# Bidirectional GRU over normalised images: statistics one image ahead of their scales, weight scaling on VectorE, three images summed raw, a shorter order decision

## What is computed

```python
# x: (16, 32, 32, 128) float32, B images of H x W tokens of C channels
xn = (x - mean(x, -1)) / sqrt(var(x, -1) + 1e-5) * ln_gamma + ln_beta
gray = xn.mean(-1)
gp = pad(gray, 1, mode='reflect')
grad_h = resize(abs(gp[..., 2:] - gp[..., :-2]))       # back to 32 x 32
grad_v = resize(abs(gp[..., 2:, :] - gp[..., :-2, :]))
scores = [avgpool3_mean(g) for g in (grad_h, grad_v, (grad_h + grad_v) / 2, abs(grad_h - grad_v))]
logits = relu(scores @ mlp_w1.T + mlp_b1) @ mlp_w2.T + mlp_b2
idx = argmax(softmax(logits))                          # per image
seq = where(idx == 1, columns_first(xn), rows_first(xn))   # (B, 1024, 128)
z = seq @ in_w.T + in_b
yf = gru(z @ wih_f.T + bih_f, whh_f, bhh_f)            # 1024 steps forward
yb = gru(z @ wih_b.T + bih_b, whh_b, bhh_b)            # 1024 steps backward
out = x + concat(yf, yb) @ out_w.T + out_b
```

## Time and profile before

| | |
|---|---|
| median of 3 runs | 1676.18 us (1672.85 to 1676.67) |
| profiled execution, its own time | 1678.4 us |
| its span, first to last instruction | 1676.6 us |
| PE busy / DVE busy / ACT busy / POOL busy | 1609.8 / 1441.4 / 1152.9 / 52.7 us |
| mean granted TensorE clock | 0.522 |
| first sigmoid of the recurrence starts | 85.19 |

### The profile page before, as it was taken

How to read it: one execution, slowest core, us unless ns; L and a number is a source line. 1 busy time by engine, 2 the same in 40 slices (tenths; PEclk the granted TensorE clock), 3 DMA queues, 4 the chain that set the end, 5 groups by cost and what they waited for, 6 DMA issues and landing times.

```text
span 1676.6 us, 61286 instructions
## 1 busy us (share of the span) xinstructions
PE 1609.8 (96%) x21671; PEld 1203.5 (72%) x21671; DVE 1441.4 (86%) x8900; ACT 1152.9 (69%) x6226; POOL 52.7 (3%) x142
## 2 busy tenths in 40 slices
PE   6799999999999999999999999999999999999997
PEld 3477777777777777777777777777777777777775
DVE  6789999888888888888888888888888888888887
ACT  6766666666666666666666666666666666666666
POOL 6500000000000000000000000000000000000000
PEclk9855555555555555555555555555555555555555
DMA  5200000000000000000000000000000000000000
GB/s 177 77 15 12 12 15 12 14 13 12 15 12 12 15 12 15 12 12 15 12 12 8 13 14 12 13 13 12 15 12 13 13 11 15 12 13 13 11 14 17
DMA packets 40359, 31.28 MB, mean 19 GB/s; under 512 B 3576, under 2 KB 37880, under 8 KB 40056
## 3 DMA queue, kind: packets, MB, share of 16 engines
q1 hardware_dynamic: 40056, 27.35, 5.6%
HBM read 18.95 MB, written 8.39 MB: 16 GB/s over the span
## 4 chain that ended last, share of the span: by engine, by line
DVE 68%; ACT 21%; issue 7%; PE 2%; POOL 1%; DMA 0%; SPq 0%; DVEq 0%; POOLq 0%
DVE state L926 31%; ACT drive L530 21%; DVE bank L915 18%; DVE halves L935 12%; DVE big L907 3%; DVE seq L891 2%; DVE xin L907 1%; POOL xin L401 1%; DVE drive L942 1%; PE bank L560 1%; PE bank L552 1%; DMA gamma_row<-in_gamma 0%; ACT seq L455 0%; PE bank L652 0%; ACT big L460 0%
## 5 line engine op out<-in xcount | busy, mean ns | idle before, releaser
L652 PEld LDWEIGHTS bank<-halves,wsplit 128*128 128x128 f16 x18432 | 648.4, 105 | 396.7 <-DVE halves L935 289.2
L652 PE MATMUL bank<-halves,wsplit 128*128 128x16 f16 x18432 | 834.3, 181 | 39.7 <-DVE halves L935 36.2
L926 DVE TENSOR_TENSOR_SCAN state<-gain,drive 128x48 f32<-128x48 f32 x2048 | 526.7, 257 | 165.2 <-ACT drive L530 15.4
L652 PE MATMUL bank<-seq,wcomb 128*128 128x128 f32 x1536 | 592.9, 482 | 2.9 <-DVE seq L891 2.9
L530 ACT ACTIVATE drive<-bank 128x16 f32<-128x16 f32 x2048 | 395.9, 193 | 267.5 <-DVE bank L915 3.0
L524 ACT ACTIVATE rpair<-bank 128x16 f32<-128x16 f32 x2048 | 380.3, 186 | 225.3 <-PE bank L652 225.3
L915 DVE TENSOR_TENSOR_SCAN bank<-rpair,bank 128x32 f32<-128x32 f32 x2048 | 453.1, 221 | 3.4 <-ACT rpair L524 3.4
L935 DVE SCALAR_TENSOR_TENSOR halves<-state 128x32 f16<-128x32 f32 x2048 | 402.9, 197 | 35.5
L527 ACT ACTIVATE gain<-bank 128x16 f32<-128x16 f32 x2048 | 394.1, 192 | 0.0
L652 PEld LDWEIGHTS bank<-seq,wcomb 128*128 128x128 f32 x1536 | 386.0, 311 | 3.1 <-DVE seq L891 3.1
L942 DVE SCALAR_TENSOR_TENSOR drive<-gain,state 128x16 f32<-128x16 f32 x2046 | 365.8, 179 | 0.0
(11 more groups left out here) (104 smaller groups left out, 186.9 us busy)
## 6 DMA issues: line engine op xcount, KB each, us to landing
xin<-in_x SPq DMA_DIRECT2D x16, 512.0 KB, 3.5
big<-in_x SPq DMA_DIRECT2D x96, 64.0 KB
out<-big SPq DMA_DIRECT2D x96, 64.0 KB
xin<-in_x SPq DMA_DIRECT2D x32, 64.0 KB
out<-xin SPq DMA_DIRECT2D x32, 64.0 KB
wih<-in_wiht SPq DMA_DIRECT2D x2, 384.0 KB, 5.9
con<-in_consts SPq DMA_DIRECT2D x1, 572.0 KB
whh<-in_whht SPq DMA_DIRECT2D x2, 192.0 KB, 7.0
```

The lines of the kernel that those rows point to most:

```text
L652: return nc.tensor.matmul(o, w, m, start=start, stop=True, skip_group_check=True)
L926: v.tensor_tensor_scan(state[:, d, ring, :], gain[:, e, cols], drive[:, e, cols], 0.0, ALU.mult, ALU.subtract).then_inc(state_ready[d], 1)
```

## The change

The diff has five groups of edits.

1. DVE's queue is statistics(n), scales(n-1) up to image 12. ACT's `deviation` moves one image further ahead, deviation(n+2).
2. N_PE is 13: images 13, 14 and 15 are summed raw, each between its statistics and its scales. The copy of gray rows is cut into two halves of 512, and stands one image earlier in ACT's queue. The last image is normalised in its own slot.
3. The squares, the high and low parts and `wcomb` move from ACT to DVE, the middle part from the decision phase to the image phase.
4. Decision: halo edges are a multiplication by a column of constants on DVE instead of two products; one bitwise operation takes the absolute value from PSUM; waits among the taps are loosened; the bias b2 is a 33rd row of the product; ACT loads the Exp table ahead of the biases; transposes(15) come behind the resize product in PE's queue; some PSUM banks change.
5. Start of the recurrence: `select` in four pieces of 8 tokens, the fills of a direction wait for its own piece, and the first step does no products on the zero state.

```diff
-N_PE = 14
+N_PE = 13
...
         act.wait_ge(eps_set, 1)
-        act.activation(table[:, :], eps[:, :], ACT.Sqrt)
-        deviation(0)
+        act.activation(table[:, 0:1], eps[:, :], ACT.Sqrt)
+        for n in range(2):
+            deviation(n)
...
         for n in range(B):
             normalise(n)
-            if n == N_PE + 1:
-                act.wait_ge(gray_mm, N_PE)
-                act.copy(gray_rows[:, :], pair[2][0:B, :]).then_inc(gray_copied, 1)
             if n > 0:
                 evacuate_rows(n - 1)
-            if n < B - 1:
-                deviation(n + 1)
+            if n + 2 < B:
+                deviation(n + 2)
             if n > 0:
                 evacuate_columns(n - 1)
-            if n == 4:
-                act.wait_ge(whh_in, 16 * N_REC)
-                act.activation(square[:, :], w_all, ACT.Square, accum_out=sums[:, 0:1]).then_inc(square_set, 1)
+            if n == N_PE:
+                for k in range(2):
+                    act.wait_ge(gray_mm, 2 * N_PE - 1 + k)
+                    act.copy(gray_rows[:, 512 * k:512 * (k + 1)], bank[4 + k][0:B, :]).then_inc(gray_copied, 1)
...
-            if n == 9:
-                act.wait_ge(scale_set, 1)
-                act.activation(parts[0], w_all, ACT.Identity, scale=sk[:, 0:1]).then_inc(high_set, 1)
-            if n == 10:
-                act.activation(parts[2], w_all, ACT.Identity, scale=sk[:, 1:2]).then_inc(weights_set, 1)
-            if n in (11, 12):
...
+        act.activation(table[:, 1:2], eps[:, :], ACT.Exp)
         act.wait_ge(bias_mm, 1)
...
-        for n in range(B):
+        for n in range(B - 1):
             transposes(n)
...
         one(halo[:, 0, :], matrix(C_LEFT), gray[:, :, TPP])
-        one(halo[:, 0, :], matrix(C_LEFT_EDGE), gray[:, :, 2], start=False)
-        one(halo[:, 1, :], matrix(C_RIGHT), gray[:, :, 1])
-        one(halo[:, 1, :], matrix(C_RIGHT_EDGE), gray[:, :, TPP - 1], start=False).then_inc(halo_mm, 1)
+        one(halo[:, 1, :], matrix(C_RIGHT), gray[:, :, 1]).then_inc(halo_mm, 1)
...
-        pe.wait_ge(seq_set, 2 * B)
+        transposes(B - 1)
+        pe.wait_ge(seq_set, 2 * B - 2)
         pooled(0, horiz, first=True)
...
-            if base + r > 0:
-                pe.wait_ge(halves_ready[d], base + r)
+            if base + r == 0:
+                return
...
+        for d in range(2):
+            pe.wait_ge(select_edge, d + 1)
+            if d == 1:
+                pe.wait_ge(reset_and_hn[0], 2)
+            fill_input(0, 0, G_R, d).then_inc(reset_pre[d], 1)
+            fill_input(0, 0, G_N, d).then_inc(reset_and_hn[d], 1)
+            if d == 1:
+                pe.wait_ge(update_ready[0], 1)
+            fill_input(0, 0, G_Z, d).then_inc(update_pre[d], 1)
         pe.wait_ge(select_done, 1)
-        for g in (G_R, G_N, G_Z):
-            fill_input(0, 0, g, 0)
-        for g in (G_R, G_N, G_Z):
-            fill_input(0, 0, g, 1)
...
+        def weight_parts():
+            w_all = whh[:, :, :].rearrange("p d n -> p (d n)")
+            parts = [wsplit[:, k].rearrange("p d n -> p (d n)") for k in range(3)]
+            v.tensor_scalar(parts[0], w_all, sk[:, 0:1], None, ALU.mult).then_inc(high_set, 1)
+            v.tensor_scalar(parts[2], w_all, sk[:, 1:2], None, ALU.mult)
+            dve.wait_ge(high_set, 1)
+            v.scalar_tensor_tensor(out=parts[1], in0=w_all, scalar=sk[:, 0:1], in1=parts[0],
+                                   op0=ALU.mult, op1=ALU.subtract).then_inc(weights_set, 1)
+
+        statistics(0)
+        for n in range(1, B + 1):
+            if n < N_PE:
+                statistics(n)
+                scales(n - 1)
+            if n == N_PE:
+                scales(n - 1)
+            if N_PE <= n < B:
+                statistics(n)
...
+                raw_gray_sums(n)
+                scales(n)
+            if n == 4:
...
+                v.scalar_tensor_tensor(out=square[:, :], in0=flat, scalar=1.0, in1=flat, op0=ALU.mult, op1=ALU.mult,
+                                       accum_out=sums[:, 0:1]).then_inc(square_set, 1)
+            if n == 9:
+                weight_scale()
+            if n == 10:
...
+                weight_parts()
+            if n == 11:
+                for d in range(2):
+                    v.tensor_scalar(wcomb[:, d, :], bank[6 + d][:, 0:3 * HID], sk[:, 0:1], None, ALU.mult).then_inc(fold_set, 1)
...
-        select(0, EDGE)
-        select(L - EDGE, L).then_inc(select_done, 1)
+        select(0, TB).then_inc(select_edge, 1)
+        select(L - TB, L).then_inc(select_edge, 1)
+        select(TB, EDGE)
+        select(L - EDGE, L - TB).then_inc(select_done, 1)
```

More of the change, by code:

```diff
@@ L146, in build @@
     eps = sb("eps", [P, 1])
-    table = sb("table", [P, 1])
+    table = sb("table", [P, 2])
     con = sb("con", [P, C_END])
@@ L247, in build @@
     terms_set = sem("terms_set")
+    taps_set = sem("taps_set")
     high_set = sem("high_set")
@@ L629, in pooled @@
                 at = C_POOL + (which * TPP + j) * 4
-                ins = one(bank[2][0:4, 0:B], con[:, at:at + 4], values[:, :, j], start=first and j == 0)
+                ins = one(bank[0][0:4, 0:B], con[:, at:at + 4], values[:, :, j], start=first and j == 0)
             return ins
-        pe.wait_ge(seq_set, 2 * B)
+        transposes(B - 1)
+        pe.wait_ge(seq_set, 2 * B - 2)
         pooled(0, horiz, first=True)
@@ L644, in _ @@
         pe.wait_ge(scores_set, 1)
[L645 removed]
+        one(bank[1][0:32, 0:B], mlp1[:, :], scores[:, :]).then_inc(hid_mm, 1)
         pe.wait_ge(terms_set, 1)
[L647 to L648 removed]
+        one(bank[1][:, P:P + 4 * B], ones[0:33, :], terms[:, :, :].rearrange("k c b -> k (c b)")).then_inc(logits_mm, 1)
+        pe.wait_ge(seq_set, 2 * B)
         def mm(o, w, m, start=False):
@@ L842, in _ @@
         dve.wait_ge(halo_mm, 1)
-        v.tensor_copy(gray[:, :, 0::TPP + 1].rearrange("p b e -> p e b"),
-                      bank[5][:, 0:2 * B].rearrange("p (e b) -> p e b", e=2)).then_inc(halo_set, 1)
-        dve.wait_ge(halo_set, 1)
+        for e in range(2):
+            v.scalar_tensor_tensor(out=gray[:, :, e * (TPP + 1)], in0=gray[:, :, 2 + e * (TPP - 3)],
+                                   scalar=con[:, C_EDGE + e:C_EDGE + e + 1], in1=bank[5][:, e * B:(e + 1) * B],
+                                   op0=ALU.mult, op1=ALU.add).then_inc(halo_set, 1)
+        dve.wait_ge(halo_set, 2)
         link(v.tensor_tensor(across, gray[:, :, 2:TPP + 2], gray[:, :, 0:TPP], ALU.subtract))
```

133 lines of the change are left out of this document (57 added, 76 removed).

## The result

| | before | after |
|---|---|---|
| median of 17 runs each | 1675.88 us (1672.85 to 1677.76) | 1678.94 us (1677.44 to 1682.85) |
| ratio, 95% interval | | 1.0024 [1.0016, 1.0031] |
| profiled execution, own time | 1678.4 us | 1679.76 us |
| its span | 1676.6 us | 1677.9 us |

The change makes the kernel slower, by 4.0 us by the ratio and 3.1 by the medians, 0.24% and less than the 0.3% that one measurement can tell from no change. The forecast was +1.6.

The account below looks back on a forecast made before the run. Only the start of the recurrence, which runs unchanged on VectorE and ScalarE, can move: image phase +4.0, decision phase -1.0 - 0.2 - 1.6 + 0.4, sum +1.6, so 1677.8 us on the median; range 1672 to 1681.5.

Parts of the forecast that it names:

- mark: Second forward step's matmuls in the recurrence, at 86.51 us before; forecast to move +1.6, with everything after it unchanged.
- ring of four slots: Image phase: scales wait for next statistics, its load and transposes three images back; 10.5 us for three images, 3.5 each.
- short start: Mask's end to the mark: smaller select, fewer fills, no products on zero states; 3.7 us instead of 5.3, -1.6.
- lies 2.2 above the median: Profiled execution of before, 1678.4 us, against median 1676.18; the +1.6 was applied to the median, giving 1677.8.
- T0: T0 to T15 are the starts of each image's transposes on TensorE; T0 is 12.28 us in the profile of before.
- T9 49.5: Image phase: image 9's transposes start at 49.5 us, the last start listed under the ring of four slots.
- The scaled copies: Weight work on VectorE: two copies of 768 elements, taken at 0.93 us each; about 0.5 by the skill page.
- -1.0: Decision phase, halo start to scores copy: 5.7 us instead of 6.7, with TensorE's own queue the long way.
- +0.4: Before ScalarE's first sigmoid: register load and branch take 1.3 to 1.4 us with 1.0 idle left, 0.4 exposed.
- The load is not the limit: Faster rival: statistics never wait for loads and VectorE's own work decides the image phase; -5.8, about 1670.4 us; chance 0.12.
- The image phase breaks even: Rival: ring and raw sums cost half of the forecast, the tail pays; +2.0 - 2.4, 1675.8 us; chance 0.24.
- TensorE stays slow or falls early: Slower rival: late full clock or a fall at 57 in the image phase; 1681 us, or 1684; chance 0.15.

Follow-up runs that it names:

- second profiles: Kernel before and changed kernel, both unedited, run and profiled again; changed kernel's ratio to before 1.0021, mark 86.17 against 85.22.
- six slots: Changed kernel with six slots for images instead of four; ratio to the kernel before 1.0004.
- old images with the new tail: Changed kernel without look-ahead, weight work on ScalarE, two images raw, scale chain at its old place; ratio to the kernel before 0.9974.
- the last kernel: Old images with the new tail, but the last image's transposes back in front of the halo products; ratio to the kernel before 1.0000.
- the second set: Second of three sets of four follow-up kernels, each set on one chip with the kernel before timed beside it; median of before 1675.35 us.

## Why the prediction was right or wrong

**The sum, step by step**, in us against the profile of before, with the two second profiles against each other in the last column:

| up to | forecast | measured | second profiles |
|---|---|---|---|
| last scaling of gray rows | +3.8 | +3.9 | +4.05 |
| weights of the halo products | +4.0 | +3.0 | +2.3 |
| copy of the scores | +3.0 | +3.4 | +3.15 |
| end of the mask | +2.8 | +3.1 | +2.6 |
| mark | +1.6 | +1.5 | +1.0 |

**Right.** The rule that only the start of the recurrence can move held: from the mark to the end of the span it took 1590.1 before and 1589.9 after, and 1589.3 and 1589.1 in the second pair. The ring of four slots is there: 10.4 from image 4 to 7 and 10.6 from 5 to 8, where 10.5 was forecast and the kernel before took 9.3 and 9.6. The wait that changes its name is in the waits of after, and the six slots show the price. The squares fell beside a wait: they ran at 20.55, and the next statistics waited for a load until 23.14. The raw sums ended at 71.24 and the scaling stood at 71.47, where 71.4 was forecast. The short start gave -1.6, as summed: 3.65 from the end of the mask to the mark, 5.27 before.

**Wrong: "lies 2.2 above the median", carried over as if common to both kernels.** This is the step that failed. The forecast for the median was 1677.8 and the median 1678.94. The profiled execution of before lay 2.5 above the median of its 17 runs and that of after 0.8. These 1.7 are what the medians' 3.1 has beyond the marks' +1.5; why the two executions lay where they did is open.

A late start isn't the reason, though it hid a term. I took T0 as unchanged at 12.28, for no reason but that row, and the diff says otherwise: the scales of image 0 now stand behind the statistics of image 1. Between the two second profiles, where GpSimd began at 7.6 before and at 9.4 after, that is 1.8 at T0. I costed T1 only (16.57 to 18.85, measured 17.64) and took +1.6 for image 2 where the two pairs have 2.1 and 2.0. But at the last scaling the pairs differ by 3.9 and 4.05, so the late start of the first profile left hardly anything of its own there.

**Luck in the sum.** The mark came to +1.5 because errors cancelled. The halo products stood at +3.0 and not +4.0, the stretch from them to the scores cost 0.4 more than before instead of 1.0 less, and the 0.4 for the register load did not appear.

**Wrong inside a right sum: "T9 49.5".** It came at 51.03. Two terms were missing. The wait of the scale chain for ScalarE's norm (1.24, with the shift of image 9 behind it) is one that the look-ahead makes: VectorE runs an image ahead and ScalarE does not. The other is GpSimd's stall. Its seven operations for image 9 took 4.43 instead of 3.05 while VectorE worked on 768 elements. Together they are 2.6, and 1.5 of it showed. The step after repaid part of it: T12 came at 61.40, where 61.7 was forecast.

**The scaled copies.** I took 0.93 each, and they took 0.61 and 0.62, 0.52 and 0.55 to the start of the next. The 0.5 that I had worked out from the Trainium skill, "VectorE: DVE Perf Modes", section on the perf-mode tier table, was the better figure.

**The stall of GpSimd.** In the eight profiles with the weight parts on VectorE the longest operation of this kind took 1138 to 1263 ns. In the six without them it took 517 to 597; in the one with the weight work on ScalarE alone, 449 up to 57.9 us and 586 later, once VectorE makes raw sums. In the old images with the new tail, a nine-column cast took 0.85 beside VectorE's 768-element operation (70.70 to 71.71), where the same cast took 0.19 or 0.20 in the last kernel, which has that operation elsewhere. The Trainium skill, "GPSIMD Engine Reference", section Specifications, says that GpSimd shares its SBUF interfaces with VectorE, with contention where VectorE runs in a 2-port performance mode or has two SBUF inputs. The traces agree: of the two slow operations in the changed kernel one lay beside the scaled copies, which read one tensor, and the other beside the third part, which reads two. The prediction did not weigh this rule, which speaks against the change.

**"-1.0" for halo products to scores.** It took 7.1 (their weight load at 73.37 to the copy at 80.50) where 6.75 was the row of before and 5.7 the forecast. The forecast's terms were added up too low: as listed they make 5.7 with every low end and 6.8 with every high end, before any hand-over, and not "5.7 to 6.0". The products ran at the lower level for most of the way, so the high ends were the ones to take. The last transposes alone took 1.92 (76.18), at the lower clock level (1.2 GHz); the stretches show it granted from 74 to 78, where before was back at 0.98 by 76:

```profile
72.00:74.00 2.00, 2.00 (x13) 1.97 (x12) 0.27 (x1) 2.00 (x4) 2.00 (x6) 0.60 0.00 0
74.00:76.00 2.00, 1.52 (x7) 1.26 (x7) 1.10 (x5) 2.00 (x3) 1.75 (x6) 0.50 0.00 0
76.00:78.00 2.00, 2.00 (x10) 1.69 (x9) 1.86 (x8) 0.19 (x1) 1.58 (x7) 0.50 0.03 8
```

But the halo products had started sooner than forecast, 1.9 behind the last scaling where I had 3.0. From that scaling to the copy of the scores the tail gained 0.5 and 0.9 in the two pairs of profiles; the forecast has 0.8. Taking the move away cost 1.2 by the marks. So moving the last transposes does gain, but by an earlier start of the halo products and not by a shorter way from them to the scores: in the old images the two stretches are 0.9 and 8.0 with the move, 4.8 and 5.9 without.

**"+0.4" for ScalarE's register load.** By the profile of after the first two fill products ended at 85.50 (84.71 and 0.79) and the first sigmoid started at 85.54, so hardly any of it was exposed. No kernel took the load away, and its own length is not measured.

**The rivals.** "The load is not the limit" fell: VectorE waited 14.5 us for loads, in 9 waits (the first images among them). "The image phase breaks even" fell: the last scaling came 3.9 later, not some 2. "TensorE stays slow or falls early" happened in part. The granted clock fell to 0.50 in 52 to 54 us, behind the 2.81 of idle time, and the gray sums took 3.48. T10 was 0.5 behind its forecast for it (55.52), and T12 no longer.

**What stays open.** The marks' differences, 1.0 and 1.5, and the medians' 3.1 agree only with each execution's offset taken off. In the second set half of the runs of before lie at 1672.9 to 1674.2 and half at 1675.4 to 1677.0, and both profiles of before were in executions of the upper half or above it. What the lower half does differently no profile shows. The sizes of single parts are no better known than this: most kernels have one profile, and differences of ratios from two chips miss those of the marks by up to some 3 us.

## What to carry to other kernels

A look-ahead on one in-order engine moves three waits, not one: the first items stand behind a later load, the ring closes over the buffers, and side work meets its producer before it is ready. Open the ring (more buffers), begin the look-ahead after the first items, and move side work behind the hand-off that others wait for; together this gave 5 to 6 us here where each alone gave 0.7 to 2.8. Before summing against one profiled execution, compare its own time with the median of many runs, and don't carry its offset over to the changed kernel. Look at its first waits too: if a load ends there late, the order of the work behind it is hidden, and a change of that order is not free.

## What the hardware showed that I had not expected

- GpSimd: beside VectorE's 768-element operations two 128-column operations took 1126 and 1141 ns instead of 449; the longest was 1138 to 1263 in all eight profiles that had the weight parts on VectorE there, and 597 at most in the six others. A nine-column cast took 854 instead of 196.
- A tensor_scalar of 768 fp32 elements to f16 took 0.61 us on VectorE; the same size with two tensors took 1.04.
- TensorE's granted clock went from 1.00 to 0.50 in the stretch that followed 3.7 us without a weight load (up to 51.0): 0.98 in 50 to 52, 0.50 (1.2 GHz) in 52 to 54, 1.00 (2.4 GHz) again from 56. At the lower level four gray products took 3.48 us instead of 1.89.
